# A graph-attention mask turned by TensorE and ScalarE instead of by DMA transposes, with the second layer's first units in another order

## The reference, cut to what matters

```python
def gat_conv(x, src, dst, W, a_src, a_dst, bias, H, C, n):
    h = (x @ W).reshape(n, H, C)
    s_src = (h * a_src).sum(-1)
    s_dst = (h * a_dst).sum(-1)
    e = jax.nn.leaky_relu(s_src[src] + s_dst[dst], NEG_SLOPE)
    emax = jax.ops.segment_max(e, dst, num_segments=n)
    ee = jnp.exp(e - emax[dst])
    denom = jax.ops.segment_sum(ee, dst, num_segments=n)
    alpha = ee / denom[dst]
    out = jax.ops.segment_sum(alpha[:, :, None] * h[src], dst, num_segments=n)
    return out.reshape(n, H * C) + bias
...
x_norm = layer_norm(x, norm_g, norm_b)
out1 = gat_conv(x_norm, src, dst, W1, a_src1, a_dst1, b1, H1, C1, N)   # 4 heads
out2 = gat_conv(out1, src, dst, W2, a_src2, a_dst2, b2, H2, C2, N)     # 2 heads of 96
return jnp.concatenate([x, out2], axis=-1) @ Wu + bu
...
q, k = elu(x @ Wq + bq) + 1, elu(x @ Wk + bk) + 1                      # the mix, 12 heads
out = ((q @ (k.T @ v)) / (q @ ksum)) @ Wo + bo
```

## Time and profile before

| | us |
|---|---|
| runs without the profiler, median (lowest, highest) | 962.59 (960.71, 964.2) |
| the profiled execution, by the clock of the runs | 964.2 |
| its span | 962.4 |
| TensorE busy in the span | 912.5 (95%) |
| VectorE busy | 746.1 (78%) |
| ScalarE busy | 350.1 (36%) |
| the stretch with the ten masks, J step 0 to the end of T step 9 | about 293 to 471 |
| layer 1's units | about 471 to 600 |
| layer 2 from its first unit to its last weights | about 637 to 691 |

### The profile page before, as it was taken

One profiled execution on the slowest core, in us unless ns is written; L12 is line 12 of the kernel. 1 busy time (PEld: TensorE's weight loads), 2 busy tenths in 40 slices (PEclk: granted clock), 3 DMA queues, 4 the chain that ended last, 5 costly groups with the idle time before them and its releaser, 6 DMA issues.

```text
span 962.4 us, 17237 instructions
## 1 busy us (share of the span) xinstructions
PE 912.5 (95%) x6379; PEld 670.4 (70%) x6381; DVE 746.1 (78%) x1704; ACT 350.1 (36%) x464; POOL 134.2 (14%) x153
## 2 busy tenths in 40 slices
PE   6899999989999999999999999989997899999995
PEld 5667676756665555567799999679866666666662
DVE  7878999997877799895889997889989544444443
ACT  5751212122235314314345552465446223232320
POOL 3400000000002000000000000020010344545441
PEclk9999999999999999999999999999998899999998
DMA  9610212246367689697792000189475668778860
GB/s 324 193 60 24 77 62 70 72 172 236 116 215 226 215 270 267 186 285 259 246 390 83 12 1 1 34 196 330 167 283 216 258 162 196 185 183 195 201 156 3
DMA packets 78844, 164.29 MB, mean 171 GB/s; under 512 B 28308, under 2 KB 47638, under 8 KB 75818
## 3 DMA queue, kind: packets, MB, share of 16 engines
q1 hardware_dynamic: 63402, 117.18, 35.9%
q0 software_dynamic: 10944, 38.22, 16.5%
q10 hardware_dynamic: 4416, 7.78, 2.2%
HBM read 109.13 MB, written 50.51 MB: 166 GB/s over the span
## 4 chain that ended last, share of the span: by engine, by line
PE 72%; DVE 18%; DMA 3%; issue 3%; ACT 2%; SPq 1%; DVEq 1%; ACTq 0%; POOLq 0%; POOL 0%
PE PS L2050 46%; PE PS L2323 15%; PE PS L2151 3%; DVE arena L1784 3%; PE PS L2521 2%; DVE arena L1611 1%; DVE arena L1432 1%; DVE arena L1617 1%; DMA arena<-in_L_ffn_W_dram 1%; PE PS L2162 1%; PE PS L2536 1%; PE PS L2342 1%; DVE arena L1594 1%; DVE arena L1497 1%; PE PS L2219 1%
## 5 line engine op out<-in xcount | busy, mean ns | idle before, releaser
L2050 PE MATMUL PS<-arena 128*128 128x384 f16 (+7 forms) x3396 | 561.5, 321 | 7.8 <-DVE arena L2040 3.0
L2050 PEld LDWEIGHTS PS<-arena 128*128 128x128 f16 (+2 forms) x3396 | 319.9, 99 | 214.3 <-issue 10.0
L2323 PE MATMUL PS<-arena 128*128 128x193 f32 (+1 forms) x1200 | 178.4, 310 | 3.2 <-DVE arena L1617 2.5
L2323 PEld LDWEIGHTS PS<-arena 128*128 128x128 f32 x1200 | 176.4, 191 | 5.3 <-DVE arena L1617 3.8
L1189 ACT ACTIVATE arena<-arena,AS 128x1250 f32<-128x1250 f32 x60 | 79.9, 1338 | 74.7 <-DVE arena L1611 74.6
L1617 DVE SCALAR_TENSOR_TENSOR arena<-arena 128x1250 f32<-128x1250 f32 x60 | 87.1, 1453 | 5.8 <-PE PS L2323 5.7
L1497 DVE TENSOR_SCALAR arena<-arena 128x240 f16<-128x240 f16 x324 | 88.8, 274 | 0.0
L1611 DVE SCALAR_TENSOR_TENSOR arena<-arena,AS 128x1250 f32<-128x1250 f32 x55 | 83.0, 1508 | 0.0
L1496 DVE TENSOR_SCALAR arena<-arena 128x128 f16<-128x128 f16 x324 | 79.8, 246 | 0.1
L2039 DVE SCALAR_TENSOR_TENSOR arena<-PS,arena 128x768 f32<-128x768 f32 x27 | 25.8, 957 | 62.6 <-PE PS L2050 62.6
L1321 ACT ACTIVATE arena<-PS 128x1536 f16<-128x1536 f16 x27 | 39.1, 1449 | 74.8 <-PE PS L2521 74.8
(11 more groups left out here) (276 smaller groups left out, 914.0 us busy)
## 6 DMA issues: line engine op xcount, KB each, us to landing
arena<-in_L_ffn_W_dram SPq DMA_DIRECT2D x48, 384.0 KB, 3.8
fr_d<-arena SPq DMA_DIRECT2D x48, 384.0 KB, 3.3
arena<-fr_d SPq DMA_DIRECT2D x16, 1152.0 KB, 12.3
arena<-in_x_dram SPq DMA_DIRECT2D x18, 384.0 KB, 5.6
arena<-rr_d SPq DMA_DIRECT2D x4, 1280.0 KB, 8.6
g_d<-arena SPq DMA_DIRECT2D x10, 388.0 KB, 2.4
acc_d<-arena SPq DMA_DIRECT2D x10, 384.0 KB, 3.4
xf_d<-arena ACTq DMA_DIRECT2D x10, 384.0 KB, 3.5
```

The costliest lines, as they stand in the source:

```text
L2050: m = T.matmul(out, left[i][x], right[i][y], start=first and i + r == 0, stop=last and 3 * i + r == n - 1)
L2323: m = T.matmul(ps[sum_bank(h, b)][:, r * (C + 1):(r + 1) * (C + 1)], (PT1 if deep == 3 else PT)[i % deep][:, d * P:(d + 1) * P], feats, st ...
```

## The change

Three things change.

First, the masks. edge_or_not writes min(count, 1), that is 1 for an edge and 0 for none. TensorE turns each piece in two halves of five 128x128 bf16 transposes into PSUM bank 3 (mask_half in the tensor block), and ScalarE reads a half out as Relu(BIG - BIG * x) into mask1 (mask_half in the scalar block), which is the old mask. Half m belongs to tile m // 2; the halves stand at the steps in HALF_J and HALF_T. On TensorE a half waits until ScalarE has read out the half before it, since both use the same bank; on ScalarE the first half of a tile waits for the maxima of the tile two before (s_max_done) and its store. SyncE loses the DMA transposes; it stores a mask after its second half.

Second, in layer 2, RELU is (0, 2, 4, 6, 8) instead of (0, 2, 5, 7, 9), no slopes stand before the weights of unit 0, and from unit 1 on the slopes run up to two units ahead through both heads.

Third, row(1) and row_out(1) stand before late_graph(2) and late_out(2).

```diff
@@ tables, semaphores
+        bigc = sb("bigc", [P, 1], F32)
-        TURN_J = {6: 5, 8: 6, 10: 7}
-        TURN_T = {0: 2, 2: 3, 3: 4, 4: 8, 6: 9}
-        STORE_J = {2: 0, 4: 1, 6: 4, 8: 5, 10: 6}
-        STORE_T = {2: 2, 3: 3, 4: 7, 6: 8, 9: 9}
+        HALF_J = {1: (0,), 2: (1,), 3: (2,), 4: (3,), 6: (10,), 7: (11,), 8: (12,), 9: (13,), 10: (14,), 11: (15,)}
+        HALF_T = {1: (4, 5), 2: (6, 7), 3: (8, 9), 5: (16, 17), 6: (18, 19)}
-        RELU = (0, 2, 5, 7, 9)
+        RELU = (0, 2, 4, 6, 8)
@@ gpsimd
+            const(g.memset(bigc[:, :], BIG))
@@ scalar
+            def mask_half(m):
+                d, c = divmod(m, 2)
+                act.wait_ge(s_mask_psum, m + 1)
+                if c == 0 and d >= 2:
+                    act.wait_ge(s_max_done, (d - 1) * H1)
+                    act.wait_ge(masks_out[d % 2], 16 * (d // 2))
+                if c == 0 and d < 2:
+                    for b in range(3):
+                        act.wait_ge(gbufs[b], 16 * ((NT + 2 - b) // 3))
+                a.activation(mask1[d % 2][:, 5 * c:5 * c + 5, :], ps[3].bitcast(BF16)[:, 0:5 * P].rearrange("p (t d) -> p t d", t=5),
+                             ACT.Relu, bias=bigc[:, :], scale=-BIG).then_inc(s_mask_ready, 1)
...
                     for c in conv_of_j[i]:
                         conv_high(c)
+                    for m in HALF_J.get(i, ()):
+                        mask_half(m)
...
                 for t in range(c0 // P, (c0 + w) // P):
+                    ms = HALF_T.get(t, ())
+                    for m in ms[0:1]:
+                        mask_half(m)
                     for c in conv_of_t[t]:
                         conv_high(c)
...
+                    for m in ms[1:]:
+                        mask_half(m)
@@ scalar, layer 2
                 row_out(0)
+                row_out(1)
                 late_out(2)
-                row_out(1)
                 late_out(3)
@@ vector
-                    dve.wait_ge(masks_in[d % 2], 16 * (d // 2))
-                V.tensor_scalar(ind1[:, d % 2, :, :], CT[:, :, d * P:(d + 1) * P], 0.0, BIG, ALU.is_equal, ALU.mult).then_inc(s_ind_ready, 1)
+                    dve.wait_ge(s_mask_psum, 2 * (d - 1))
+                V.tensor_scalar(ind1[:, d % 2, :, :], CT[:, :, d * P:(d + 1) * P], 1.0, None, ALU.min).then_inc(s_ind_ready, 1)
...
-                        dve.wait_ge(masks_in[d % 2], 16 * (d // 2 + 1))
+                        dve.wait_ge(s_mask_ready, 2 * (d + 1))
...
-                    while ahead < len(SLOPED) and SLOPED[ahead] <= i + (2 if 0 < i < NT else 1):
+                    while i and ahead < len(SLOPED) and SLOPED[ahead] <= i + 2:
@@ tensor
+            def mask_half(m):
+                d, c = divmod(m, 2)
+                pe.wait_ge(s_ind_ready, d + 1)
+                if m:
+                    pe.wait_ge(s_mask_ready, m)
+                else:
+                    pe.wait_ge(s_cols_ready, 1)
+                for t in range(5 * c, 5 * c + 5):
+                    k = T.transpose(ps[3].bitcast(BF16)[:, (t - 5 * c) * P:(t - 5 * c + 1) * P], ind1[:, d % 2, t, :], identb[:, :])
+                k.then_inc(s_mask_psum, 1)
...
             row(0)
+            row(1)
             late_graph(2)
-            row(1)
             late_graph(3)
```

More of the change, by code:

```diff
@@ L719, in xa_store, with mask_stores @@
                 sp.dma_start(acc_d[t * P:(t + 1) * P, :], XA[t % 2]).then_inc(xa_out[t % 2], 16)
[L721 to L730 removed]
+            def mask_stores(halves):
+                for m in halves:
+                    if m % 2:
+                        d = m // 2
+                        sp.wait_ge(s_mask_ready, m + 1)
+                        sp.dma_start(mask_d[:, d * NP:(d + 1) * NP], mask1[d % 2].rearrange("p t d -> p (t d)")).then_inc(masks_out[d % 2], 16)
             for c in range(2):
@@ L765, in _ @@
             sp.dma_start(bias_d.rearrange("(a n) -> a n", a=1), brow[0:1, :]).then_inc(s_small_in, 16)
-            for d in range(2):
-                mask_turned(d)
             def rr_load(h):
@@ L1693, in _ @@
                         assert t == t0 + 1 and not ns
-                        for b in range(2):
-                            dve.wait_ge(masks_in[b], 16 * ((NT + 1 - b) // 2))
+                        dve.wait_ge(s_mask_psum, 2 * NT)
                         dve.wait_ge(s_rows_ready, 1)
@@ L2301, in _ @@
                 shared(i + 5)
+                ms = HALF_T.get(t + 1, ())
+                for m in ms[0:1]:
+                    mask_half(m)
                 mixed_part(t, c0, 2, KC)
+                for m in ms[1:]:
+                    mask_half(m)
                 mixed_part(t + 1, c0, 0, KC)
                 for t in range(t + 2, (c0 + w) // P):
+                    ms = HALF_T.get(t, ())
                     if t in LATER:
-                        mixed_part(t, c0, 0, KC)
+                        for m in ms[0:1]:
+                            mask_half(m)
+                        mixed_part(t, c0, 0, KC // 2)
+                        for m in ms[1:]:
+                            mask_half(m)
+                        mixed_part(t, c0, KC // 2, KC)
                         continue
                     for c in range(2):
+                        if c < len(ms):
+                            mask_half(ms[c])
                         graph_part(t, c)
```

30 lines of the change are left out of this document (8 added, 22 removed).

## The result

The changed kernel takes 971.76 us (median of 6 runs, 970.45 to 977.25) where the kernel before, timed beside it, takes 964.06 (6 runs, 960.71 to 964.83). The ratio is 1.0098 with a 95% interval of 1.008 to 1.0116. All 32 executions of the changed kernel on record from the first occasion took 969.4 to 977.25 us, with a median of 972.8, so its first median lies low rather than high. The forecast was 968.5 us and +5.9 us, in a range of 963.5 to 973.5. So the sign is right and the time lies in the range, but the loss is 7 to 9 us and not 6, and the two terms that make the difference are named at the end.

The account below looks back on a forecast made before the run. TensorE was taken to bound the mask stretch, VectorE mostly layer 2. Masks +5.0 us and layer 2 +0.9 us made +5.9 us, from the median 962.6 to 968.5 us; range 963.5 to 973.5.

Parts of the forecast that it names:

- The bound: Mask stretch: TensorE, idle 1.86 of 178.0 us, pays for added transposes at 0.057 us each, 0.28 a half, 5.0 us.
- The two free halves: T steps 0 and 4: the first half fits in about 0.3 us of waiting for VectorE, so costs nothing.
- ScalarE's read-outs at zero: Masks: 20 read-outs of 0.78 us on ScalarE, 1.9 us spare a J step, cost TensorE zero; bounds 0 and 5 us.
- Rival 2: Masks: TensorE waits for ScalarE's read-outs, 3 to 10 us more, 971.5 to 978.5 us; chance 0.13.
- What is removed: Masks: DMA transposes leave SyncE and the queues, buying TensorE at most a share of 1.86 us; room for weight loads.
- The start of layer 2: Exponential 0 ends at 638.4, when weights 0 can begin; aggregate 0 at 639.9, aggregate 1 at 646.1, 0.4 us later.
- +2 if the clock falls at the first idle time: Layer 2: upper bound on its +0.9 us, for late graphs running slow after TensorE's first idle time.
- The units: Layer 2: slopes and weights at 1.40 us each on VectorE; weights end at 691.9, last aggregate 0.9 us later.
- The wait of a us ahead of the last weights: Layer 2's end: three weights stand in a row and the last waits 1.2 us for aggregate 17.
- The sum: Masks 5.0 us and layer 2 0.9 us make +5.9 us, 968.5 us on the median's scale.
- Rival 1: Layer 2 gives back 2.2 to 4.4 us of VectorE's idle time, 963.2 to 965.4 us in all; chance 0.20.
- rival 5: Layer 2: unit 8 needs the last accumulating DMA 2.3 us earlier; up to 2.3 us lost, inside the forecast's range.

Follow-up runs that it names:

- e11: The changed kernel with each of the 100 mask transposes made twice; 977.4 us, ratio 1.0117 to the kernel before.
- e7: The kernel before with only the layer 2 changes (RELU list, slopes' condition, row order), a second timing; 967.28 us, ratio 1.0032.
- e13: The changed kernel with row(1) and row_out(1) back behind late_graph(2) and late_out(2); 969.98 us, ratio 1.0051 to the kernel before.
- e2: The kernel before with only the layer 2 changes (RELU list, slopes' condition, row order), first timing; 964.22 us, ratio 1.0012.
- e6: The kernel before with only the masks changed, layer 2 in its old order, a second timing; 968.2 us, ratio 1.0049.
- e10: The kernel before with 22 idle matmuls (result unused) ahead of row(2); 964.33 us, ratio 0.9985.
- e3: The kernel before with only the RELU list and the slopes' condition changed, rows in their old order; 963.91 us, ratio 1.0005.
- e16: The kernel before with 22 idle matmuls ahead of row(2) and four in each of two idle times ending layer 1; 962.76 us, ratio 0.9981.
- e8: The changed kernel with the second head's slopes only one unit ahead of the weights; 970.82 us, ratio 1.0077 to the kernel before.
- e12: The changed kernel with each mask half read out of PSUM twice on ScalarE; 977.38 us, ratio 1.0125 to the kernel before.

## Why the prediction was right or wrong

- **The bound.** Right. TensorE was busy for all but 1.86 of 178 us, and 18 halves of 0.28 came out as +4.84 us for 5.0. The distance between starts was the right price, not the recorded 219 ns: e11 adds 0.28 us a half and 4.94 in all. The about 275 ns of the Trainium skill that were weighed there (TensorE: Matmul & The Clock Gate, "Part 4: PE-mode transpose") are of the size of the recorded duration, 219 ns; as a cost they are too high by a factor of almost five here (57 ns).
- **The two free halves.** The sum fits: 4.84 is 17 to 18 halves of 0.27 to 0.28. In the changed kernel the half of T step 0 stands at 333.62, and the mixed parts behind it start at 333.90 without the wait that they had before.
- **ScalarE's read-outs at zero.** Right in its sum, by a thinner margin than its working said. The J steps bore 0.8 us more a half without a stall; in T steps 2 and 6 the cover is 0.4 us and nothing, since those read-outs wait for maxima, a wait that stands in the description of the change and that the working did not price. Rival 2 did not come.
- **What is removed.** Right for TensorE, which gets nothing of it: its idle time in the window went from 1.86 to 1.16 us. ScalarE waits 25 us less for weights, and 23 us for what its new read-outs need.
- **The start of layer 2.** Right where the clock held. In e7, which has no mask change, aggregates 0 and 1 start at 640.07 and 646.30, by the forecast 639.9 and 646.1. In the changed kernel this step failed, and it is the larger part of the miss, 1.7 us. The prediction let exponential 0 end at 638.4, just when weights 0 can begin, and took that as free of charge; it left no slack for a slow stretch of TensorE and put the low clock into a bound ("+2 if the clock falls at the first idle time") instead of the sum. The bound was near in size (+1.7) and wrong in its place: the clock fell at 621, ahead of any of the new idle times. It came in both profiles of the changed kernel, and in every other with its masks. Whether the changed masks call it, by moving the stage or by what they add, no run tells; that the moved row makes it cost something, e13 shows.
- **The units.** This term failed too, by 0.9 us. "Slopes and weights take 1.40 each" was read from the old order, in which a slopes never overwrites what the weights just before it read. In the new one it does, at 0.12 us a pair, in 8 pairs; in the trace 7 of them show it, since the denominators stand between the two in the eighth. That is 0.84 us, and in e7, on the scale of before, the weights end at 692.78 where the prediction had 691.9. With it 0.9 becomes 1.7 to 1.8, and e2 and e7 measure 1.84. The wait of a us ahead of the last weights was forecast and came.
- **The sum.** 4.84 + 1.84 + 1.7 is 8.4 for the stages in place of 5.9; the comparison of medians gives 7.4 to 7.7, the ratios 7.4 to 9.4. The nearness of the forecast to the medians may owe something to luck: the profile of before, from which the terms were read, had a slow row(2) that made the new order look about a us cheaper in stage 2 than it is beside e6. Rival 1 was wrong in its sign: VectorE's idle time did not shrink into a gain. Of rival 5, late sums, no wait was seen.

## What to carry to other kernels

Price an added instruction by the distance between starts in a row of its kind, and where TensorE has no idle time, take the full sum. When slopes of any kind are moved further ahead through a ring of buffers, count which instruction frees the buffer: if it is the one just issued on the same engine, each step pays for its completion. An order that sends a small chain between two engines earlier can take away slack that used to swallow a slow stretch of TensorE; ask of each moved wait what it absorbed.

## What the runs showed of the hardware that I had not expected

TensorE's clock fell to 0.50 for 3 to 4 us at a time between 609 and 626, while it was busy and its last idle times had been two of 0.4 us: from 610 to 625 on end in e10, once in the changed kernel, not at all in e2 and e7. The work just ahead was narrow, twenty matmuls of two columns. In the profile of before the fall at 637 followed an idle time of 2.92 us, and I had tied the one to the other. The runs neither refute nor settle that: the fall came again in e3, the only other profile with that idle time, and is gone in e10 and e16, which fill it. But an idle time is not needed, as the falls from 609 on show, and shorter ones decide nothing: behind the 2.02 us ahead of row(1) in the moved order the clock fell in e8, e11 and e12 and stayed in seven others. And a wait of VectorE for its own preceding instruction costs 0.12 us (1.49 us from start to start instead of 1.37) without appearing in the view of waits.
